# Holding GpSimd's scatters until the product of the denominators

## The reference, cut to what matters

```python
q_prime = exp(q @ proj.T); k_prime = exp(k @ proj.T)
D = einsum('bhnf,bhf->bhn', q_prime, k_prime.sum(2))     # the denominators
context = einsum('bhmf,bhmd->bhfd', k_prime, v)
out = einsum('bhnf,bhfd->bhnd', q_prime, context) / (D + 1e-6)
h = h + out @ Wout.T + bout
x = layernorm(h)                                         # then the experts
topv, topi = top_k(x @ Wg, 2);  w = softmax(topv)
y = sum over e of gw[..., e] * ((silu(x @ W[e]) * (x @ V[e])) @ W2[e])
```

## Time and profile before

| | us |
|---|---|
| median of 3 runs | 1214.05 |
| the runs | 1208.42 to 1215.71 |
| the profiled execution, its own time | 1208.1 |
| its span, first to last instruction | 1206.3 |
| mean granted clock of TensorE, of full speed | 0.976 |

### The profile page before, as it was taken

How to read it: one execution, slowest core, us unless ns; L and a number is a source line. 1 busy time by engine, 2 the same in 40 slices (tenths; PEclk the granted TensorE clock), 3 DMA queues, 4 the chain that set the end, 5 groups by cost and what they waited for, 6 DMA issues and landing times.

```text
span 1206.3 us, 30227 instructions
## 1 busy us (share of the span) xinstructions
PE 1119.9 (93%) x8672; PEld 949.0 (79%) x8673; DVE 878.5 (73%) x3310; ACT 561.3 (47%) x1307; POOL 627.1 (52%) x656
## 2 busy tenths in 40 slices
PE   4899999899899899999998779999999999999996
PEld 4577667667677676676666558999999999999995
DVE  6477777777687777776875656777777777777774
ACT  3534435436345354354333213555555555555552
POOL 0014435344444344354443544677777777777675
PEclk9899999999999899999999989999999999999999
DMA  8160201210301202110010313344344444444442
GB/s 179 39 178 26 76 24 35 71 31 29 75 31 37 62 29 68 35 33 27 28 31 22 89 49 84 48 59 54 51 54 53 58 53 55 53 54 55 56 55 29
DMA packets 76010, 65.58 MB, mean 54 GB/s; under 512 B 12339, under 2 KB 66803, under 8 KB 75927
## 3 DMA queue, kind: packets, MB, share of 16 engines
q0 software_dynamic: 32704, 24.99, 14.8%
q1 hardware_dynamic: 41990, 38.71, 12.9%
q10 hardware_dynamic: 1232, 0.85, 0.3%
HBM read 32.81 MB, written 31.71 MB: 53 GB/s over the span
## 4 chain that ended last, share of the span: by engine, by line
PE 67%; DVE 16%; issue 5%; another core or an unknown queue 4%; DMA 2%; POOL 2%; ACT 1%; SPq 1%; POOLq 0%; DVEq 0%; ACTq 0%
PE bank L1356 20%; PE bank L1368 13%; PE bank L647 5%; PE bank L698 4%; DVE patches L798 3%; PE bank L685 3%; PE bank L711 3%; PE bank L687 3%; PE bank L686 3%; PE bank L704 2%; DVE rparts L888 2%; PE bank L447 2%; PE bank L585 2%; DVE rden L876 2%
## 5 line engine op out<-in xcount | busy, mean ns | idle before, releaser
L1483 POOL DMA_INDIRECT out_rows<-yo,dest x184 | 327.6, 1780 | 135.6 <-issue 89.4
L1356 PE MATMUL bank<-xT_e,wv 128*128 128x256 f32 x2208 | 287.0, 285 | 0.9 <-DVE xT_e L1433 0.9
L1356 PEld LDWEIGHTS bank<-xT_e,wv 128*128 128x128 f32 x2208 | 270.1, 189 | 1.2 <-DVE xT_e L1433 1.2
L1245 POOL DMA_INDIRECT sorted_rows<-xrow_all,sloti x192 | 190.0, 990 | 62.3 <-issue 52.3
L1407 ACT ACTIVATE sil<-bank 128x256 f32<-128x256 f32 x368 | 141.1, 384 | 160.8 <-PE bank L1356 141.4
L1368 PE MATMUL bank<-w,hid 128*128 x1472 | 179.7, 275 | 2.7 <-DVE hid L1440 2.7
L1368 PEld LDWEIGHTS bank<-w,hid 128*128 128x128 f32 x1472 | 171.5, 192 | 3.2 <-issue 3.2
L1440 DVE TENSOR_TENSOR hid<-sil,bank 128x256 f32<-128x256 f32 x368 | 145.0, 417 | 25.1 <-ACT sil L1407 22.2
L1422 DVE TENSOR_TENSOR wv<-wv_all,wv 128x1024 fp32r<-128x1024 f32 x92 | 112.7, 1225 | 67.7 <-issue 36.3
L1160 ACT ACTIVATE attn<-bank 128x256 f32<-128x256 f32 x128 | 49.3, 386 | 196.2 <-PE bank L687 164.8
L1391 ACT CAST wv<-wv_all 128x1024 fp32r x92 | 96.2, 1046 | 39.0 <-issue 39.0
(11 more groups left out here) (191 smaller groups left out, 1936.2 us busy)
## 6 DMA issues: line engine op xcount, KB each, us to landing
xr<-sorted_rows SPq DMA_DIRECT2D x92, 130.0 KB
raw<-in_x SPq DMA_DIRECT2D x64, 84.5 KB
raw<-in_x SPq DMA_DIRECT2D x60, 78.0 KB
out_rows<-attn SPq DMA_DIRECT2D x64, 58.5 KB
sorted_rows<-xrow_all,sloti POOLq DMA_INDIRECT x192
out_rows<-yo,dest POOLq DMA_INDIRECT x184
wv_all<-in_L_ffn_W SPq DMA_DIRECT2D x8, 256.0 KB, 5.6
wv_all<-in_L_ffn_V SPq DMA_DIRECT2D x8, 256.0 KB, 5.7
```

The costliest lines, as they stand in the source:

```text
L1245: po.indirect_dma_start(sorted_rows, bass.IndirectOffsetOnAxis(sloti[:, p, j, ch:ch + 1], 0), xrow[:, p, j, ch], None).then_inc(s(f"scatte ...
L1356: q = pe.matmul(bank[fc][:, TT * m:TT * m + TT], wv[:, w, w_, m, cols], xT[:, p, x_], start=(w_ + x_ == 0), stop=(w_ == 1))
L1483: po.indirect_dma_start(out, bass.IndirectOffsetOnAxis(dest[:, p, a:a + 1], 0), yo[:, p, a], None, compute_op=ALU.add).then_inc(s(f"added{ ...
```

## The change

Three edits, all in POOL's program of a step:
1. In steps 4 to 31 the scatters of pair n - 4 wait for `d8_done` of `md + 2` = n - 1, which is the product of this very step. Before, they waited for `md + 1` = n - 2, the product of the step before.
2. Pairs 28 and 29 are now scattered like the others, one step later than before: in steps 32 and 33, behind the product of that step. These steps have no first root; in its place stands a wait until the first three scatters have landed (the count of 48).
3. Pair 30 (step 33) and pair 31 (step 34) are scattered in their own step as before, but both now have two scatters ahead of the place of the root and four behind it. In step 33 that is the last root; before, four scatters stood ahead of it and two behind.

```diff
-                if a and n > 3:
-                    wait_alone(po, setup_met, (s("sloti_ready"), md), (s("w1_ready"), md), (s("d8_done"), md + 1))
+                if 3 < n < NPAIR + 2:
+                    wait_alone(po, setup_met, (s("sloti_ready"), md), (s("w1_ready"), md), (s("d8_done"), md + 2))
                     scatter(range(1), 1 - pd)
                     scatter(range(1, 2), 1 - pd, (0,))
                 if a:
                     ...  # the first root
-                if a and n > 3:
+                if 3 < n < NPAIR + 2:
+                    if not a:
+                        po.wait_ge(s(f"scattered{1 - pd}"), 96 * ((md - 1) // 2) + 48)
                     scatter(range(1, 2), 1 - pd, (1,))
                     scatter(range(2, NCH), 1 - pd)
-                late = n + 1 < NPAIR
-                before_root = {NPAIR: 3, NPAIR + 1: 2}.get(n, 1)
+                late = n < NPAIR + 1
...
                 if d and not late:
                     wait_alone(po, setup_met, (s("sloti_ready"), md + 1), (s("w1_ready"), md + 1))
-                    scatter(range(before_root))
+                    scatter(range(1))
                 if c:
...
                 if d and not late:
                     wait_alone(po, setup_met, (s("sloti_ready"), md + 1))
-                    scatter(range(before_root, NCH))
+                    scatter(range(1, NCH))
```

## The result

| | before | after |
|---|---|---|
| median, us | 1214.88 (4 runs, 1208.42 to 1216.46) | 1157.39 (4 runs, 1154.57 to 1161.96) |
| ratio, 95% interval | | 0.954, 0.949 to 0.959 |
| profiled execution, us | 1208.1 | 1159.45 |
| its span, us | 1206.3 | 1157.6 |
| mean granted clock | 0.976 | 0.991 |

The forecast was 1165.8 us, the range 1153 to 1190. All lines behind L1258 have moved down by one. "+x" is again the time from a step's L578.

The account below looks back on a forecast made before the run. PE, busy 93%, was taken as the bound, idling in 15 steps behind held `d8_done` updates. Edit 1's 48.0 us plus 0.3 from edits 2 and 3 gave 48.3 off 1214.05: 1165.8 us, range 1153 to 1190.

Parts of the forecast that it names:

- Edit 1: Steps 6 to 31: no scatter starts before this step's product updates, so `dsum` comes at +0.9; 48.0 us off.
- a scatter that begins: Claimed that a scatter beginning while the narrow product (L578) runs holds back its `d8_done` update by 1.8 to 4.5 us.
- the count of 15: Steps with k = 2 and 3 from 6 to 27, and 29 to 31: scatter starts inside the product, `dsum` waits on "remote".
- Edit 2: Step 32: no scatter lies over L711 any more, so its held update and the next product come 3.3 us earlier.
- Edit 3 and the tail: Step 33's product to first tile: last root 0.5 later, two more scatters behind it 2.5; 3.0 us later in all.
- The landing of three scatters: POOL's wait in step 33: start to landing taken as about 2.5 us, between bounds of 1 and 4.7.
- I carry the same saving over: From the profiled 1159.8 us to the median: the same 48.3 us saving off 1214.05 gives 1165.8 us.
- A part only: Held updates go, but DVE stands still per scatter in 15 steps or clock stays 0.93; 1181 to 1191 us; chance 0.11.
- Nothing: The scatter's start is no cause of the late update; only the tail's 3.0 us is added, 1217 us; chance 0.07.
- Slower: Any scatter beside PE holds updates; 15 steps keep their cost, 13 others get 2.35 us each; 1248 us; chance 0.04.

Follow-up runs that it names:

- the run with one scatter ahead: Changed kernel with a step's first scatter waiting only for the last step's product, the others for this step's: 1176.2 us (1 run).
- the experiment on it: Changed kernel with a pair's sixth scatter kept until the first quarter of L711 is done, so it begins inside L711's products: 1160.1 us (1 run).

## Why the prediction came out

**Edit 1, right, in mechanism and size.** The scatter's start at +1.6 (measured +1.65), `dsum` at +0.9 (+0.86 to +0.95), k = 2 at 19.40 (19.37 in most, 19.73 in step 22), k = 3 at 19.5 (19.48 to 19.56), steps 29 to 31 at 55.23 (55.26), a clock of 1.00 over both stretches: each term came from the length of a twin step that wasn't held, and that carried the clock's share along without its being priced apart. 48.0 forecast, 47.3 measured. The order as the trigger is shown by the run with one scatter ahead. Two things were missing in it. It is a trigger only on some chips; on the others the kernel before has nothing to gain, and the two halves of the change gave 0.1% there, inside their intervals (the changed kernel as a whole wasn't run on one of those). And "a scatter that begins" was too little: the scatters behind it help to set how long the hold lasts (1.1 us with one, 2.5 with three, in step 29). One row was misread: step 32 does have an early scatter, at +1.46. It begins behind the product, so the count of 15 stands.

**Edit 2, the mechanism partly, the size not.** -3.3 was forecast for step 32 and -6.8 came. The update of L711 is no longer late, 3.3 as forecast. The remaining 3.5 goes with the clock, which was 0.80 before and for which I had no term: the profile after has 1.00 in this step, and PE's busy time fell from 17.05 to 13.88 with the same 117 products. That isn't steady, though: in the second profile of the changed kernel the clock was 0.84 and the step took 20.78, so this step saves 4.5 to 6.8. Nor is it shown that the edit was needed for it: with edit 1 alone, on chips without the hold-up, the step took 19.02 and 20.67. The general form of the reason, any scatter over L711, fell with the experiment on it.

**Edit 3 and the tail, right in sum, by luck.** +3.0 forecast, +2.91 measured. The last scatter is 5.05 later after step 33's product, near the upper bound of 5.5: the root 1.7 later and not 0.5, and 3.3 for the rest in place of 2.5. Against that stand 2.1 us less between the last scatter and the first tile (4.70 to 2.56), for which I had no term. It is no accident of one profile: this gap is 4.5 to 5.8 us in all nine profiles with the old tail and 2.6 to 2.9 in all five with the new one. Why, no run shows. And most of the +2.91 isn't the edit's price. In the seven profiles with the old tail and no late update the stretch was already 32.9 to 34.2 us, against 31.05 in the earlier trace rows's profile and 33.96 now: before, step 33's product itself came 3.3 us late, and POOL's chain didn't come late with it. My sum charged this to the scatters. The landing of three scatters, taken as 2.5 from a start, was 2.6 (from 661.63 to 664.26).

**The start-up, no term.** +2.67 up to step 6, of which 2.60 are there at step 2 already (L578 at 63.78 in place of 61.18), where the change does nothing yet; the other profiles have it anywhere from 61.1 to 66.4. It is what single executions differ by.

**From the profiled run to the median.** The profiled execution was forecast at 1159.8 and took 1159.45. The error of 8.4 us lies in the last step, "I carry the same saving over": the profiled execution of the kernel before was faster than all four of its runs (1208.1 against 1208.42 to 1216.46), while the changed kernel's was above its median. The ordinary runs saved 57.5 us and the profiled pair 48.7; on the second such chip 54.1.

**The rivals.** *A part only*, DVE standing still for a whole scatter: no, L888 takes 0.97 to 1.06 beside one and 0.83 without, and L894, which reads two tensors, 0.99 to 1.00 either way. The Trainium skill's lock (SBUF — State Buffer, section "SBUF: two separate sides") would have left 1.0 us in each step; these rows show a stretch of 0.14 to 0.23. The page ties the lock to conditions that my forecast left out (a vector instruction in a mode that uses two ports, or one with two inputs beside a GpSimd instruction that reads SBUF), and no run shows which of them hold here. So the rows show no lock at work, and don't contradict the page. *Nothing*: no. But there is a second condition beside the scatter's start, it differs from chip to chip, and no term of the prediction allowed for it. The same section's sentence that PE never waits on anyone is about ports of SBUF. It fits PE's own starts, which follow one another without a gap behind a held product; it doesn't cover when PE's update arrives. *Slower*: no, L906 starts at +3.99 in step 29 of the changed kernel (587.65), with two scatters over the products before it.

## What to carry to other kernels

A wait that ends on "remote" while its releaser has long ended is worth a table of all such steps against what else began at that moment; here it named the trigger and, by the steps without it, the gain in these steps to within 1 us. Price a removed stall by the length of a step of the same work that hasn't got it, since this takes in the clock and what comes next. Where a stretch starts at an event that was itself late, as the tail here, look first at what it measures when the event is on time. And run the unchanged kernel on several chips before a gain is written down: this change is worth 4.5% on some, and on others neither of its halves gave anything that could be measured.

## What the runs showed of the hardware

- The kernel before took 1213 to 1215 us in two groups of runs (the prediction's and one of the experiments', which may be one chip or two) and 1159 to 1163 on three other chips. In step 29 the scatter starts at +0.48 or +0.49 on either kind, and `dsum` at +3.45 or at +0.95.
- One indirect DMA on POOL that began 0.48 us into 32 narrow matmuls delayed their update by 1.1 us, three in a row by 2.5 (step 29, on one chip); one inside the 64-column products of L711 delayed nothing there.
- Even on a chip of the second kind step 30 had `dsum` 0.6 late (+1.54), the step that is held longest (+5.46) on the first. A full-width product that carried the update there didn't spare it (+1.55 and +1.57, 0.3 later than in the steps beside it), a copy of 0.81 us on POOL inside the product in place of the scatter did (+0.94 and +0.95).
- Between the last scatter's start and the load that waits for its landing passed 4.5 to 5.8 us in the nine profiles with the old order of the last scatters and 2.6 to 2.9 in the five with the new one.
